# Decoder layer on one core: expert outputs added to the attention sums in memory by accumulating DMAs

## The reference

```
X = X + ctx @ wo
h2 = rmsnorm(X, norm2_w).reshape(B * S, d)
logits = h2 @ router_w
...
shared = swiglu(h2, sh_gate, sh_up, sh_down)
gate = jnp.einsum('td,edf->etf', h2, e_gate)
up = jnp.einsum('td,edf->etf', h2, e_up)
eout = jnp.einsum('etf,efd->etd', jax.nn.silu(gate) * up, e_down)
spec = jnp.einsum('etd,te->td', eout, combine)
moe_out = (shared + spec).reshape(B, S, d)
return X + moe_out
```

## Time and profile before

| | us |
|---|---|
| median of 3 runs | 1203.14 |
| lowest, highest | 1200.74, 1205.42 |
| the profiled execution, its time | 1210.79 |
| its span (first to last instruction) | 1209.0 |

### The profile page before, as it was taken

One profiled execution on the slowest core, in us unless ns is written; L12 is line 12 of the kernel. 1 busy time (PEld: TensorE's weight loads), 2 busy tenths in 40 slices (PEclk: granted clock), 3 DMA queues, 4 the chain that ended last, 5 costly groups with the idle time before them and its releaser, 6 DMA issues. The chain is left out here.

```text
span 1209.0 us, 32884 instructions
## 1 busy us (share of the span) xinstructions
PE 1082.4 (90%) x13012; PEld 1015.5 (84%) x13012; DVE 810.2 (67%) x1383; ACT 622.7 (52%) x1264; POOL 588.4 (49%) x631
## 2 busy tenths in 40 slices
PE   3799999999999999999728988799999999999981
PEld 2578888899899888898628987799999999999981
DVE  1668877878778778776535432477677767767576
ACT  1245455565555555665422232466666666666443
POOL 4243433433444343334101666267767766766555
PEclk8999999999999999999957988899999999999995
DMA  7585465454555554410058222256766676676265
GB/s 202 97 188 106 80 123 107 90 116 115 108 96 118 116 98 88 86 43 20 28 180 317 88 84 88 100 202 222 244 232 210 226 247 225 217 248 225 86 194 174
DMA packets 288456, 176.37 MB, mean 146 GB/s; under 512 B 213120, under 2 KB 256896, under 8 KB 287680
## 3 DMA queue, kind: packets, MB, share of 16 engines
q1 hardware_dynamic: 277600, 148.90, 46.1%
q0 software_dynamic: 6816, 18.69, 4.3%
q10 hardware_dynamic: 3888, 6.69, 1.5%
HBM read 130.25 MB, written 54.28 MB: 153 GB/s over the span
## 5 line engine op out<-in xcount | busy, mean ns | idle before, releaser
L1395 DVE TENSOR_TENSOR prod<-silu,up 128x512 f32<-128x512 f32 x110 | 75.1, 683 | 161.4 <-ACT silu L1249 139.2
L1379 DVE TENSOR_TENSOR we_lo<-w_raw,we_hi 128x1024 fp32r<-128x1024 f32 x117 | 148.0, 1304 | 15.3 <-ACT we_hi L1233 12.0
L1516 POOL TENSOR_TENSOR act_lo<-prod,act_hi 128x512 fp32r<-128x512 f32 x78 | 100.6, 1290 | 101.5 <-ACT act_hi L1256 101.5
L1524 POOL DMA_INDIRECT routed_scratch<-y_rows,slot_place x78 | 130.9, 1678 | 21.2 <-issue 14.7
L1249 ACT ACTIVATE silu<-gate 128x512 f32<-128x512 f32 x110 | 64.9, 590 | 128.2 <-PE up L1180 98.1
L1233 ACT ACTIVATE we_hi<-w_raw 128x1024 fp32r<-128x1024 f32 x117 | 118.1, 1049 | 21.7 <-DMA w_raw<-in_w_down 21.6
L1256 ACT ACTIVATE act_hi<-prod 128x512 fp32r<-128x512 f32 x110 | 69.6, 632 | 89.4 <-DVE prod L1395 87.5
L668 ACT ACTIVATE p3t<-psum 128x512 f32<-128x512 f32 x128 | 68.7, 596 | 90.8 <-PE psum L517 90.8
L1483 POOL DMA_INDIRECT slots_scratch<-h_rows,slot_index x64 | 65.0, 1016 | 52.5 <-PE up L1180 33.5
L920 POOL TENSOR_TENSOR ctx_lo<-ctx_t,ctx_hi 128x512 fp32r<-128x512 f32 x16 | 20.6, 1286 | 140.3 <-ACT ctx_hi L578 140.3
L839 DVE TENSOR_REDUCE max<-psum 128x16 f32<-128x2048 f32 x32 | 73.3, 2291 | 18.2 <-PE psum L503 18.2
(11 more groups left out here) (264 smaller groups left out, 3322.5 us busy)
## 6 DMA issues: line engine op xcount, KB each, us to landing
w_raw<-in_w_gate SPq DMA_DIRECT2D x40, 512.0 KB
w_raw<-in_w_up SPq DMA_DIRECT2D x40, 512.0 KB
w_raw<-in_w_down SPq DMA_DIRECT2D x40, 512.0 KB
slots_scratch<-in_empty SPq DMA_DIRECT2D x39, 258.0 KB, 3.4
slot_rows<-slots_scratch SPq DMA_DIRECT2D x39, 258.0 KB
w_raw<-routed_scratch SPq DMA_DIRECT2D x32, 256.0 KB, 3.8
x_t<-in_x_t SPq DMA_DIRECT2D x16, 256.0 KB, 3.5
q_scratch<-qk SPq DMA_DIRECT2D x16, 256.0 KB, 2.7
```

Of the source, the lines that this page charges most:

```text
L1379: dve.tensor_tensor(w_lo[:, kind, :], w_raw[:, use % 2, kind, :], w_hi[:, kind, :].bitcast(F32), ALU.subtract).then_inc(w_lo_done, 1)
L1395: dve.tensor_tensor(prod[:, h, :], silu[:, h, :], up[h][:, :], ALU.mult).then_inc(prod_done, 1)
L1516: pool.tensor_tensor(act_lo[:, n % 2, h * FH:(h + 1) * FH, :], prod[:, h, :].rearrange("p (f n) -> p f n", f=FH), act_hi[:, n % 2, h * FH: ...
L1524: pool.indirect_dma_start(out=scratch["routed"], out_offset=bass.IndirectOffsetOnAxis(ap=slot_place[:, i % METAS, j:j + 1], axis=0), in_=y ...
```

## The change

- The attention sums stay in memory, in `total` (one row of 256 floats for each token, row 32 p + b for token p of batch b; slots without a token have rows of their own behind them). The 8 loads into `acc` are gone.
- The first 11 shared units write their results to `acc` by a copy instead of an add.
- `store_tile` becomes `add_tile`: the same two indirect DMAs of 128 rows, now with `compute_op=ALU.add`, to the token's row of `total`. First and second choices go to the same row, so POOL waits before each tile's DMAs until both of the tile before have landed. One semaphore, `y_added`, takes the place of the three `y_stored`. `second_choice` no longer sets the row number (one POOL instruction less for each of its 8 groups).
- The tail loads `total` once: 4 DMAs, the first for pairs 11 to 15 into `acc`, the others for pairs 0 to 10, four pairs each, into `front` (the space of `w_raw`). For pairs 11 to 15 `read_down` adds the shared result to the loaded total; for pairs 0 to 10 POOL adds `front` to `acc`. DVE has no add of its own left in `moments`. SP issues the output DMAs instead of ACT. `read_down` comes later in the last shared units, and FINISHED and NORMALIZED have other numbers.

```diff
-FINISHED = (0, 0, 3, 6, 9)
-NORMALIZED = (0, 0, 0, 4, 6)
+FINISHED = (0, 0, 3, 7, 12)
+NORMALIZED = (0, 0, 0, 2, 6)
...
-                for g in range(GROUPS):
-                    sp.dma_start(acc[:, g * GB:(g + 1) * GB, :], scratch["x2_x3"][:, g * GB:(g + 1) * GB, :])\
-                      .then_inc(acc_loaded, 16)
...
-                for i in range(3):
-                    sp.wait_ge(y_stored[i], 16 * 2 * len(range(i, TILES, 3)))
+                sp.wait_ge(y_added, 16 * 2 * TILES)
                 sp.wait_ge(w_lo_done, split_count(AFTER_TILES - 1, 2))
+                for g, pairs in enumerate(TOTALS):
+                    rows = slice(2 * pairs[0], 2 * pairs[-1] + 2)
+                    sp.dma_start((front if g else acc)[:, rows, :], totals[:, rows, :]).then_inc(total_loaded[g], 16)
                 for pair in range(PAIRS):
-                    if pair >= RING:
-                        sp.wait_ge(added, pair - RING + 1)
-                    load_picked(pair)
+                    sp.wait_ge(norm_done, pair + 1)
+                    sp.dma_start(out[:, 2 * pair:2 * pair + 2, :], acc[:, 2 * pair:2 * pair + 2, :]).then_inc(out_stored, 16)
...
-                        act.wait_ge(norm_done, pair + 1)
-                        act.dma_start(out[:, 2 * pair:2 * pair + 2, :], acc[:, 2 * pair:2 * pair + 2, :]).then_inc(out_stored, 16)
...
-                        dve.tensor_tensor(pair, src, pair, ALU.add).then_inc(down_read, 1)
+                        if n < FIRST_TILE:
+                            dve.tensor_copy(pair, src).then_inc(down_read, 1)
+                        else:
+                            dve.wait_ge(total_loaded[0], 16)
+                            dve.tensor_tensor(pair, src, pair, ALU.add).then_inc(down_read, 1)
                     else:
                         if i >= 3:
-                            dve.wait_ge(y_stored[i % 3], 16 * 2 * (i // 3))
+                            dve.wait_ge(y_added, 16 * 2 * (i - 2))
...
+                    if n == AFTER_TILES:
+                        read_down(n - 2)
                     product(n, 0)
-                    if 2 <= n and n - 2 != AFTER_TILES - 1:
+                    if 2 <= n < AFTER_TILES:
                         read_down(n - 2)
...
                     late = n - AFTER_TILES
+                    if late >= 2:
+                        read_down(n - 2)
                     if late >= 1:
                         finish(range(FINISHED[late - 1], FINISHED[late]))
...
-                    pool.tensor_scalar(h_rows[:, b, D], place[:, b], float(B * S), None, ALU.add).then_inc(pool_set, 1)
...
-                def store_tile(i):
+                def add_tile(i):
+
                     pool.wait_ge(down_read, FIRST_TILE + i + 1)
                     pool.wait_ge(meta_done, 2 * i + 2)
+                    if i > 0:
+                        pool.wait_ge(y_added, 16 * 2 * i)
                     for j in range(2):
                         pool.indirect_dma_start(
-                            out=scratch["routed"], out_offset=bass.IndirectOffsetOnAxis(ap=slot_place[:, i % METAS, j:j + 1], axis=0),
-                            in_=y_rows[:, i % 3, j, :], in_offset=None).then_inc(y_stored[i % 3], 16)
+                            out=scratch["total"], out_offset=bass.IndirectOffsetOnAxis(ap=slot_place[:, i % METAS, j:j + 1], axis=0),
+                            in_=y_rows[:, i % 3, j, :], in_offset=None, compute_op=ALU.add).then_inc(y_added, 16)
...
                 for pair in range(PAIRS):
-                    pool.wait_ge(picked_loaded[pair % RING], 16 * (2 * (pair // RING) + 3))
-                    first = picked[:, pair % RING, 0, :, :]
-                    pool.tensor_tensor(first, first, picked[:, pair % RING, 1, :, :], ALU.add).then_inc(combined, 1)
+                    if pair < FIRST_TILE:
+                        both = slice(2 * pair, 2 * pair + 2)
+                        pool.wait_ge(total_loaded[1 + pair // 4], 16)
+                        pool.wait_ge(down_read, pair + 1)
+                        pool.tensor_tensor(acc[:, both, :], front[:, both, :], acc[:, both, :], ALU.add).then_inc(combined, 1)
```

More of the change, by code:

```diff
@@ L1042, in phase_b @@
         down_ready, down_read = sem("down_ready"), sem("down_read")
-        y_stored = [sem(f"y_stored{i}") for i in range(3)]
+        y_added = sem("y_added")
         route, route_max, route_exp, ratio_ready, ratio_exp = (
@@ L1048, in phase_b @@
         scattered = [sem(f"scattered{i}") for i in range(2)]
-        picked_loaded = h_loaded[0:RING]
+        TOTALS = [range(BEFORE, PAIRS), *(range(i, min(i + 4, BEFORE)) for i in range(0, BEFORE, 4))]
+        total_loaded = [sem(f"total_loaded{g}") for g in range(len(TOTALS))]
         meta_done = sem("meta_done")
-        combined, added, var_done, eps_b_done, rstd_b_done, norm_done, out_stored = (
-            sem(n) for n in ("combined", "added", "var_done", "eps_b_done", "rstd_b_done", "norm_done", "out_stored"))
+        combined, var_done, eps_b_done, rstd_b_done, norm_done, out_stored = (
+            sem(n) for n in ("combined", "var_done", "eps_b_done", "rstd_b_done", "norm_done", "out_stored"))
         KINDS = ("w_gate", "w_up", "w_down")
@@ L1070, in split_count @@
             return kind + 1 if i is None else 3 + 3 * i + kind + 1
+        totals = scratch["total"][0:P * B, :].rearrange("(p b) d -> p b d", p=P)
         def low_products(k):
@@ L1128, in _ @@
                     load_expert(i + 2)
-                def load_picked(pair):
-                    for which in range(2):
-                        first = ROWS + which * B * S + 2 * S * pair
-                        rows = scratch["routed"][first:first + 2 * S, :].rearrange("(b p) d -> p b d", p=P)
-                        sp.dma_start(picked[:, pair % RING, which, :, :], rows).then_inc(picked_loaded[pair % RING], 16)
-                for i in range(3):
-                    sp.wait_ge(y_stored[i], 16 * 2 * len(range(i, TILES, 3)))
+                sp.wait_ge(y_added, 16 * 2 * TILES)
                 sp.wait_ge(w_lo_done, split_count(AFTER_TILES - 1, 2))
+                for g, pairs in enumerate(TOTALS):
+                    rows = slice(2 * pairs[0], 2 * pairs[-1] + 2)
+                    sp.dma_start((front if g else acc)[:, rows, :], totals[:, rows, :]).then_inc(total_loaded[g], 16)
                 for pair in range(PAIRS):
-                    if pair >= RING:
-                        sp.wait_ge(added, pair - RING + 1)
-                    load_picked(pair)
+                    sp.wait_ge(norm_done, pair + 1)
+                    sp.dma_start(out[:, 2 * pair:2 * pair + 2, :], acc[:, 2 * pair:2 * pair + 2, :]).then_inc(out_stored, 16)
                 sp.wait_ge(out_stored, 16 * PAIRS)
@@ L1417, in read_down, with moments @@
                         ins.then_inc(down_read, 1)
-                def add_picked(pair):
-                    dve.wait_ge(combined, pair + 1)
-                    dve.wait_ge(down_read, (pair if pair < FIRST_TILE else pair + TILES) + 1)
-                    rows = acc[:, 2 * pair:2 * pair + 2, :]
-                    dve.tensor_tensor(rows, picked[:, pair % RING, 0, :, :], rows, ALU.add).then_inc(added, 1)
-                    dve.wait_ge(added, pair + 1)
+                def moments(pair):
+                    if pair < FIRST_TILE:
+                        dve.wait_ge(combined, pair + 1)
+                    else:
+                        dve.wait_ge(down_read, pair + TILES + 1)
                     for n in range(2 * pair, 2 * pair + 2):
@@ L1433, in finish @@
                     for pair in pairs:
-                        add_picked(pair)
+                        moments(pair)
                 choose()
@@ L1532, in _ @@
                     if i >= 2:
-                        store_tile(i - 2)
+                        add_tile(i - 2)
                     if i + 1 < TILES:
@@ L1536, in _ @@
                     routed_lo(n, 1)
-                store_tile(TILES - 2)
-                store_tile(TILES - 1)
+                add_tile(TILES - 2)
+                add_tile(TILES - 1)
                 def root(pair):
```

21 lines of the change are left out of this document (9 added, 12 removed).

## The result

| | before | after |
|---|---|---|
| median us, timed side by side (4 runs each) | 1203.28 | 1187.45 |
| lowest, highest | 1200.74, 1205.42 | 1186.11, 1190.29 |
| ratio, 95% interval | | 0.9885 [0.9858, 0.9913] |
| the profiled execution, its time | 1210.79 | 1186.11 |
| its span | 1209.0 | 1184.3 |

(The ratio on record is not the quotient of the two medians, which is 0.9868. By the ratio, the 1203.14 that the forecast starts from becomes 1189.3, just inside the range.) Two later measurements, each on one chip beside the kernel before, gave 0.9948 [0.9928, 0.9968] and 0.991 [0.9892, 0.9928]. So the size of the gain depends on the measurement, and the first task was to separate what belongs to the change from what does not.

The account below looks back on a forecast made before the run. PE, busy for 90% of the span, was taken as the bound, with the weight loads almost level. The terms -0.3 + 0 + 6 - 10.5 = -4.8 us took 1203.1 to 1198.3 us, range 1189 to 1217.

Parts of the forecast that it names:

- Start of phase B: Before the tiles: removing the acc loads costs nothing, the dropped POOL instruction gives -0.3 us, at most -2.2.
- A wait on POOL: Tile units: waiting for the previous tile's DMAs, 0.5 to 2 us each, costed at 0; free up to 2.5 us.
- rival B: First DMA of each tile: the wait on POOL becomes the bound beyond 2.5 us of lateness; 1218 us, chance 0.18.
- Rival C: Tile units: POOL's DMA instruction doubles, 2.8 us a tile against 2.3 of idle; +12 us, 1210, chance 0.05.
- Traffic: Tile units: the adds' second read loads the DMA engines that carry the weights; +6 us, between +3.2 and +13.
- The tail: After the tiles: five things move, together -10.5 us, with -12.5 if DVE runs ahead and -4 if totals come late.
- (1): Tail: last tiles' adds follow each other, SP's loads of totals start at 1143 to 1148; cover some 4 us.
- (4): Tail: ACT takes two pairs instead of four before unit 54's silu and issues no output DMAs; about 3 us less.
- (5): The end, from PE's last down product: POOL sets the pace, 18.1 us instead of 25.8, so -7.7.
- (2): Tail: DVE's 16 adds of 0.833 us, 13.3 us, are gone.
- (3): Tail: POOL adds 11 pairs instead of 16, none of the last five.
- rival A: Tile units: adds as cheap as writes, the load hides the read; about 1192 us, range 1188 to 1195, chance 0.27.

Follow-up runs that it names:

- e1: Changed kernel with a POOL instruction of the dropped kind and size put back in each of the 8 scatter groups; ratio to the kernel before 0.9918.
- e2: Changed kernel with the 8 loads of acc and DVE's wait for them put back; ratio to the kernel before 0.9943.
- series 3: Third set of runs on one chip beside the kernel before (1200.74 us): r2, e7, e9 and a kernel with twelve shared units first and adds shared with DVE.
- e4: Kernel before, plain writes kept, with POOL waiting before each tile's DMAs until those of the tile before have landed; ratio to the kernel before 1.0002.
- e3: Changed kernel with plain writes in place of the accumulating DMAs, waits kept; ratio to the kernel before 0.9921.
- b1: Kernel before, unchanged, run again for a second profile; one run, 1216.05 us.
- r1: Changed kernel, nothing altered, measured again; ratio to the kernel before 0.9948.
- r2: Changed kernel, nothing altered, measured a third time; 1190.37 us, ratio to the kernel before 0.991.
- e5: Changed kernel with the output DMAs issued by ACT again instead of SP; ratio to the kernel before 0.9977.
- series 2: Second set of runs on one chip beside the kernel before: b1, e4, e5 and the changed kernel with twelve shared units ahead of the tiles.
- e7: Changed kernel with one more 128x512 DVE operation ahead of each pair's moments; 1201.17 us, ratio to the kernel before 1.0.
- e9: Changed kernel with a POOL add of 128x512 put back for each of the last five pairs; ratio to the kernel before 0.9939.
- series 1: First set of follow-up runs on one chip beside the kernel before: r1, e1, e2 and e3.

## Why the prediction was right, and where it was not

The direction was right, and the likeliest time, 1198.3, was 11 us above the first measurement's median and 5.5 above what all three measurements give.

- **Start of phase B** (-0.3): right to call it nothing. e1 and e2 put both removals back and no time came with them. The 16 us that the first profile of after gained here go with PE's stops, which other profiles of the same kernel have. The "same 6 us" of waiting for the slot rows was not a fixed figure either: 3.7 to 16.0 us in profiles of the changed kernel. In series 3 the medians fit an early first tile for the kernel before as well: 1200.74 less 1.8 around the span, less a tail of 93.5 and a tile stage of 350 to 358, leaves 747 to 755. No profile of before on that chip shows it. The same sum from 1203.28, the median of before in the first measurement, leaves 750 to 758, earlier than the 763.4 of its profile.
- **A wait on POOL, costed at nothing:** right in the price and in the size of the wait, not in its threshold. Forecast were 0.5 to 2 us each; measured 2.0 on average, longest 3.5, and PE never waits for POOL's low part. e4 shows the same for the wait alone, with shorter waits of 1.3 us. The prediction, and rival B with it, had waits above 2.5 us cost 39 us for each us, and the longest waits did not: behind 2.40 us of waiting and 1.05 us of growth of the two instructions, 3.45 us together, 1.4 us of the cover of 2.57 are left, and as much behind 3.54 us. What was left out is that POOL also stood idle ahead of that low part, so a delay eats this idle time first. One sign that was set down came: "if its instruction takes over 2 us". In after 27 of the 78 do, up to 2.61 us (before 1.80 for the first of a tile), and it cost nothing that shows. The sign beside it, a landing of over 9 us, did not come in after, with at most 8.6 us from the issue of a tile's second DMA to the end of the wait for it, and once, with 9.3, in e1. Rival C's sum has a slip: 2.8 us against 2.3 of idle time are 0.5 us too many and not 0.3, so 20 us and not 12.
- **Traffic, +6:** this is the step that failed, "I take +6". The adds did raise the queue's share, and no 6 us followed: e3 has the same tile stage without them (356.5 us against 355.4). The Trainium skill, Collectives: The Full Stack, "The bandwidth ceiling: the fold count and why AG ≠ RS ≠ AR", has two source reads for each chunk that a ReduceScatter reduces. The trace fits that in so far as the share more than doubles (7.2% to 17.3%); the time that it would give, the upper half of my range, did not come. How much of the 6 us is there stays open. From the issue of a tile's last load to the start of ACT's work on it, where ACT waited for it, the medians are 6.3 to 7.0 us in the four profiles with plain writes (before, b1, e4, e3) and 6.6 to 7.2 in six with adds (after, r1, r2, e1, e2, e5). The tile stage averages 354.2 us in the four and 356.9 in the six. With a spread of 350.5 to 357.7 inside the first group these 2.7 us are not shown to belong to the change; nor are they shown to be nothing.
- **The tail, -10.5:** measured 81.1 - 93.5 = -12.4, near the upper end of the -12.5 to -4. The sum was nearly right and its parts were not. (1) SP's loads started 31.5 us after the last transposes (1135.02 - 1103.5), forecast 27.5 to 32.5; no wait of DVE: right. (4) "About 3 us less" for PE: wrong. PE's last product waits 4.02 us, now because `finish` of four pairs stands ahead of DVE's product and itself waits 1.4 us for POOL's add. Behind it comes a low part of 1.76 us where 0.69 is usual, and then the read of unit 52 (L1406), which the change moved behind that low part and which is what releases PE. From the last transposes to it are 63.0 us, as before. (5) 18.1 us after it were forecast, 15.1 came: -10.7 instead of -7.7. Four of POOL's adds were priced here, at its pace, and only one was left; POOL had run ahead and waited for DVE. And 1.9 us came from the end, which no step has: from the last normalisation to the end of the span 2.7 us, before 4.6. That the missing 3 us of (4) and these two made up for each other is luck.

  What the parts are worth the runs of series 2 and 3 show. (2) was listed as "gone" and given no price of its own, since POOL was to set the pace. e7 prices it at 10.2 us, more than any other part; (3) is 3.0 by e9, and the output DMAs on ACT 3.0 by e5. Each was put back by itself, and together they make 16.2, more than 12.4. Whether the parts overlap or something was lost against them was not taken apart.

So rival A, "adds as cheap as writes", with 0.27, comes nearest: by its own sum 1192, and -10.3 us is the mean of the three measurements (-13.8, -6.3, -10.8 by their ratios). From 1203.14 that is 1193. They spread over more than the difference between A and the forecast: 1189, 1197 and 1192. The tail alone gives -12.4, so 2 us are left for a cost of the tile stage or for chance. The 1187.45 of the first measurement is lower than the tail by itself explains; its medians are 15.8 us apart, and its profile of after has an early first tile. Rivals B, C and D did not occur: the waits never reached PE, the instruction grew by 0.5 us each, not by double, and the tail gave more, not less.

## What to carry to other kernels

A wait that is added to an engine cost nothing here, because the engine had idle time both ahead of the next instruction that somebody needs and behind it; add up both, they stand in the rows. A larger share of the DMA engines need not cost anything by itself: ask whether the load that others wait for lands later. Where three engines hand a pair round in a ring (add, moments, root, add), don't name one as the pace by its own busy time: put the work of each back in turn and measure. And profile a kernel twice before a stage's difference of 1% is given to a change: the first tile, ahead of which the change did next to nothing, moved by 23 us between profiles.

## What the runs showed of the hardware

- An accumulating indirect DMA of 128 rows of 1 KB costs POOL 1.55 us to issue where nothing competes, a plain one 0.96. In the tail SP's loads, which wait for the last one, start 1135.02 - 1131.26 = 3.8 us after its issue began; before it was 1141.92 - 1139.31 = 2.6:

```profile
1139.31 0.96 POOL L1524 DMA_INDIRECT routed_scratch<-y_rows,slot_place  x1 [0.30 <-issue]
```

  It moves 288 packets a tile where the plain write moves 96 of three times the size.
- DVE's operations with two operands in SBUF are stretched while POOL adds; the moments, with one, are not. In the tail of after, beside POOL's adds:

```profile
1151.80 2.55 POOL L1557 TENSOR_TENSOR acc<-w_raw,acc 128x512 f32<-128x512 f32 x2
...
1153.26 1.64 DVE L1393 TENSOR_TENSOR act_lo<-prod,act_hi 128x512 fp32r<-128x512 f32 x1 [0.70 <-ACT act_hi L1252]
...
1159.70 0.76 DVE L1421 BATCH_NORM_STATS2 stats_b<-acc 128x6 f32<-128x256 f32 x2 [1.41 <-POOL acc L1557]
```

  The same operation takes 0.69 us alone, and the moments 0.72 to 0.75. This can be a part of why DVE's adds were worth more than their 0.66 us: the 16 of before took 0.833 each. The Trainium skill, GPSIMD Engine Reference, "Specifications", says that POOL shares its SBUF interfaces with VectorE, with contention for instructions with two SBUF inputs; the trace agrees.
- Between 650 and 760 us PE stopped up to 29 times in a profile, for up to 1.7 us each, with nothing shown that it waits for, 0 to 18 us in all. Profiles of one series are alike in that: the stops are there and the first tile comes at 763 to 771 in series 1 and 2, there are none and it comes at 748 to 751 in series 3. What causes it was not found.
